# A three-layer interaction network on one core: products made in pairs, one whole group fewer per step

## What is computed

```python
h = x
for i, S in enumerate([128, 128, 128]):
    Wr = Ws[i].reshape(39, h.shape[1], S)
    out = relu(einsum('bfd,bgd,fgs->bsd', x, h, Wr) + bs[i][None, :, None])
    if i != 2:
        h, direct = (out[:, :64], out[:, 64:])
    else:
        direct = out
    outs.append(direct)
return sum(concatenate(outs, axis=1), axis=-1)
```

## Time and profile before

| | us |
|---|---|
| median of 3 runs | 571.18 (571.01 to 573.93) |
| profiled execution, its time | 570.96 |
| its span in the trace | 569.1 |
| PE busy | 558.0 (98%) |
| DVE busy | 531.8 (93%) |
| POOL busy | 505.5 (89%) |
| ACT busy | 365.8 (64%) |
| granted TensorE clock, mean | 0.996 |

### The profile page before, as it was taken

How to read it: one execution, slowest core, us unless ns; L and a number is a source line. 1 busy time by engine, 2 the same in 40 slices (tenths; PEclk the granted TensorE clock), 3 DMA queues, 4 the chain that set the end, 5 groups by cost and what they waited for, 6 DMA issues and landing times.

```text
span 569.1 us, 7814 instructions
## 1 busy us (share of the span) xinstructions
PE 558.0 (98%) x2003; PEld 377.6 (66%) x2003; DVE 531.8 (93%) x516; ACT 365.8 (64%) x409; POOL 505.5 (89%) x222
## 2 busy tenths in 40 slices
PE   8899999999999999999999999999999999999997
PEld 4354666767676666667767667676767766666765
DVE  5679999999999999999999999999999999999975
ACT  1255775766767576676776758586676757668562
POOL 1257999899999999999899999989999999999995
PEclk9899999999999999999999999999999999999999
DMA  8998935738375582846649285573837558262001
GB/s 331 412 413 329 383 115 181 299 124 332 101 261 225 179 332 85 311 157 203 276 146 346 68 295 214 166 313 113 329 111 256 229 173 337 79 210 80 0 2 37
DMA packets 27390, 121.68 MB, mean 214 GB/s; under 512 B 3312, under 2 KB 3440, under 8 KB 25328
## 3 DMA queue, kind: packets, MB, share of 16 engines
q1 hardware_dynamic: 27376, 121.52, 58.8%
HBM read 120.98 MB, written 0.52 MB: 213 GB/s over the span
## 4 chain that ended last, share of the span: by engine, by line
PE 88%; POOL 5%; issue 3%; DMA 1%; DVE 1%; ACT 1%; SPq 0%; POOLq 0%; DVEq 0%; ACTq 0%
PE acc L572 88%; POOL z_lo L294 4%; DMA xfirst<-x 1%; POOL w_lo L540 1%; DVE z_whole L431 0%; DVE z_raw L431 0%; ACT h L660 0%; ACT last L660 0%; ACT z_hi L657 0%; SPq L304 0%; SPq L327 0%; DVE z_hi L292 0%; ACT direct L660 0%; DVE sums L454 0%; DVE z_lo L291 0%
## 5 line engine op out<-in xcount | busy, mean ns | idle before, releaser
L294 POOL TENSOR_TENSOR z_lo<-z_raw,z_hi 128x1024 fp32r<-128x1024 f32 x202 | 477.8, 2406 | 25.2 <-ACT z_hi L657 22.7
L657 ACT CAST z_hi<-z_raw 128x1024 fp32r<-128x1024 f32 (+1 forms) x215 | 216.9, 1022 | 111.5 <-DVE z_raw L431 94.0
L431 DVE TENSOR_TENSOR z_raw<-h,xwide 128x1024 f32<-128x1024 f32 x189 | 225.6, 1214 | 4.7 <-ACT h L660 3.0
L572 PE MATMUL acc<-z_hi,w_hi 128*128 128x512 f32 (+1 forms) x543 | 210.1, 460 | 0.8 <-ACT last L660 0.8
L572 PE MATMUL acc<-z_hi,w_lo 128*128 128x512 f32 x530 | 171.7, 395 | 0.0
L572 PE MATMUL acc<-z_lo,w_hi 128*128 128x512 f32 x498 | 160.0, 397 | 2.3 <-POOL z_lo L294 1.9
L572 PEld LDWEIGHTS acc<-z_hi,w_hi 128*128 128x128 f32 (+1 forms) x543 | 102.2, 188 | 60.6 <-issue 39.5
L572 PE MATMUL acc<-z_whole,w_whole 128*128 128x512 f32 x256 | 120.0, 592 | 0.0
L572 PEld LDWEIGHTS acc<-z_hi,w_lo 128*128 128x128 f32 x530 | 99.4, 188 | 24.0
L572 PEld LDWEIGHTS acc<-z_lo,w_hi 128*128 128x128 f32 x498 | 92.6, 187 | 28.4 <-POOL z_lo L294 5.8
L431 DVE TENSOR_TENSOR z_whole<-h,xwide 128x1024 f32<-128x1024 f32 x68 | 82.3, 1213 | 6.2 <-PE acc L572 3.9
(11 more groups left out here) (25 smaller groups left out, 155.1 us busy)
## 6 DMA issues: line engine op xcount, KB each, us to landing
xwide<-x SPq DMA_DIRECT2D x160, 512.0 KB, 4.7
xfirst<-x SPq DMA_DIRECT2D x13, 2048.0 KB, 7.8
xfirst<-x SPq DMA_DIRECT2D x4, 768.0 KB, 12.2
xwide<-w SPq DMA_DIRECT2D x2, 1024.0 KB, 16.7
xwide<-x SPq DMA_DIRECT2D x1, 1280.0 KB, 11.8
xfirst<-x SPq DMA_DIRECT2D x2, 512.0 KB, 11.4
xwide<-x SPq DMA_DIRECT2D x1, 768.0 KB, 9.2
z_raw<-w0b SPq DMA_DIRECT2D x1, 640.0 KB, 6.0
```

The costliest lines, as they stand in the source:

```text
L294: return eng.tensor_tensor(lo[0:rows, 0:n, :], z[0:rows, 0:n, :], hi[0:rows, 0:n, :].bitcast(F32), ALU.subtract)
L431: nc.vector.tensor_tensor(dst, in0, in1, ALU.mult).then_inc(made[kind], 1)
L572: return nc.tensor.matmul(dst, w[0:rows, place, :], z[0:rows, t - G * g, :], start=first and first_g and t == G * g, stop=final and t == T ...
L657: nc.scalar.copy(z_hi[0:rows, slot("PV", pair, par, pos, HI_RING), 0:n, :], src).then_inc(hi_made, 1)
```

## The change

The order of a step becomes a string in which P groups of one layer stand side by side. Two neighbouring P groups of layer 1 or 2, the first of them with an even count of P groups ahead of it, are multiplied by one DVE instruction of 2048 columns; it waits until both slots of z_raw are free and counts as two. A step now has 5 W, 14 P and 5 V groups: in layer 1 group 12 is whole, 11 is P and 13 is V (before, 11 and 13 were whole and 12 was P); in layer 2 groups 22 and 28 are whole and 25 is V. z_hi has 4 slots instead of 6. The loop body is four steps. The first steps get new orders; layer 0 of block 1 is summed in acc[2] instead of acc[0]; the split of the weights of layer 2 stands on ACT ahead of relu1 of step 1 instead of behind it; the reductions move to positions 6 and 9. On SP the load of layer 2's weights moves one place forward, ahead of the second part of block 2's x, and of the x pieces of layer 1 in step 1 five instead of six go out first. relu2 stays at position 3, relu1 at 0, relu0 at 21.

```diff
+LOOP = 4
-KINDS = ("WPWP", "PWPWPPVPPV", "PPWPVPPWPV") 
+ORDER = "10P 11P 12W 13V 14P 15P 00W 20P 21P 16V 22W 01P 02W 03P 23P 24P 25V 17P 18P 19V 26P 27P 28W 29V"
-SCHEDULE = "111112100122221001212222"
-ORDER_0 = "00W 01W 02W 03W 11W 13W 10W 12W 16W 14P 17W 15P 18P 19V"
-ORDER_1 = ("00W 01W 22W 27W 02W 03W 20P 10P 11W 21P 12P 23P 13W 14P 24V 15P 16V 25P 17P 18P 19V "
-           "26P 28P 29V")
-SPLIT2_AT_1 = 2
-WHOLE_RING, RAW_RING, HI_RING, LO_RING = 4, 4, 6, 4 
+ORDER_0 = "00W 01W 02W 03W 12W 10W 11W 13W 16W 14W 15P 17W 18P 19V"
+ORDER_1 = ("00W 01W 22W 28W 02W 03W 20P 21P 10P 11P 12W 13V 23P 24P 14P 15P 16V 25V 17P 18P 19V "
+           "26P 27P 29V")
+SPLIT2_AT_1 = 0
+WHOLE_RING, RAW_RING, HI_RING, LO_RING = 4, 4, 4, 4 
-SUM1_AT = 7
-SUM2_AT = 8
+SUM1_AT = 6
+SUM2_AT = 9
+def twin(j, pos):
+    these = order(j)[pos:pos + 2]
+    return len(these) == 2 and these[0][2] == these[1][2] == "P" and these[0][0] == these[1][0] > 0 \
+        and these[0][1] + 1 == these[1][1] and before("P", j if isinstance(j, int) else 3, pos) % 2 == 0
...
+                both = 2 if twin(j, pos) else 1
+                n = G * both if both > 1 else len(tiles_of(layer, g))
...
-                    ready(dve, lo_made["P"], number - RAW_RING + 1)
-                    dst = z_raw[0:rows, slot("P", pair, par, pos, RAW_RING), 0:n, :]
+                    ready(dve, lo_made["P"], number + both - RAW_RING)
+                    at = slot("P", pair, par, pos, RAW_RING)
+                    dst = z_raw[0:rows, at:at + both].rearrange("p a g n -> p (a g) n")[:, 0:n, :]
...
-                nc.vector.tensor_tensor(dst, in0, in1, ALU.mult).then_inc(made[kind], 1)
+                nc.vector.tensor_tensor(dst, in0, in1, ALU.mult).then_inc(made[kind], both)
...
-                    products(pair, par, pos)
+                    if not (pos and twin(j, pos - 1)):
+                        products(pair, par, pos)
...
-            with dve.Fori(1, PAIRS - 1) as pair:
-                for par in range(2):
-                    step(pair, par)
+            with dve.Fori(0, (BLOCKS - 4) // LOOP) as turn:
+                for par in range(LOOP):
+                    step(LOOP // 2 * turn + 1, par)
...
-                dst = acc[layer][:, :]
+                dst = acc[2 if isinstance(j, int) and (layer, j) == (0, 0) else layer][:, :]
...
-                    ready(pe, acc_read[layer], j + (1, 0, -1)[layer])
+                    if isinstance(j, int) and (layer, j) == (2, 1):
+                        pe.wait_ge(acc_read[0], 2)
+                    if isinstance(j, int) and layer == 0 and j < 2:
+                        ready(pe, acc_read[0], j)
+                    else:
+                        ready(pe, acc_read[layer], j + (1, 0, -1)[layer])
...
                 if isinstance(j, int) and j == 0:
-                    relu0(j, par)
                     copy_xrep(1)
+                    relu0(j, par % 2)
```

More of the change, by code:

```diff
@@ L20 @@
 PAIRS = BLOCKS // 2
+LOOP = 4
+assert LOOP % 2 == 0 and (BLOCKS - 4) % LOOP == 0
 BB = N // DIM
@@ L31, with groups @@
 TILES = (T0, T12, T12)
-KINDS = ("WPWP", "PWPWPPVPPV", "PPWPVPPWPV")
-G12 = len(KINDS[1])
-SCHEDULE = "111112100122221001212222"
-ORDER_0 = "00W 01W 02W 03W 11W 13W 10W 12W 16W 14P 17W 15P 18P 19V"
-ORDER_1 = ("00W 01W 22W 27W 02W 03W 20P 10P 11W 21P 12P 23P 13W 14P 24V 15P 16V 25P 17P 18P 19V "
-           "26P 28P 29V")
-SPLIT2_AT_1 = 2
-WHOLE_RING, RAW_RING, HI_RING, LO_RING = 4, 4, 6, 4
+ORDER = "10P 11P 12W 13V 14P 15P 00W 20P 21P 16V 22W 01P 02W 03P 23P 24P 25V 17P 18P 19V 26P 27P 28W 29V"
+ORDER_0 = "00W 01W 02W 03W 12W 10W 11W 13W 16W 14W 15P 17W 18P 19V"
+ORDER_1 = ("00W 01W 22W 28W 02W 03W 20P 21P 10P 11P 12W 13V 23P 24P 14P 15P 16V 25V 17P 18P 19V "
+           "26P 27P 29V")
+def groups(text):
+    return [(int(e[0]), int(e[1]), e[2]) for e in text.split()]
+STEP = groups(ORDER)
+KINDS = ["".join(e[2] for e in sorted(STEP) if e[0] == layer) for layer in range(3)]
+G12 = len(KINDS[1])
+SPLIT2_AT_1 = 0
+WHOLE_RING, RAW_RING, HI_RING, LO_RING = 4, 4, 4, 4
 V_LAG = 2
@@ L56 @@
 RELU2_AT = 3
-SUM1_AT = 7
-SUM2_AT = 8
+SUM1_AT = 6
+SUM2_AT = 9
 assert KINDS[1][-1] == KINDS[2][-1] == "V"
[L63 to L74, removed]
 BEGIN = {-1: [(0, g, "W") for g in range(len(KINDS[0]))],
-         0: [(int(e[0]), int(e[1]), e[2]) for e in ORDER_0.split()],
-         1: [(int(e[0]), int(e[1]), e[2]) for e in ORDER_1.split()]}
+         0: groups(ORDER_0),
+         1: groups(ORDER_1)}
 def order(j):
@@ L176 @@
 assert sorted(e[:2] for e in BEGIN[0]) == sorted(e[:2] for e in STEP if e[0] < 2)
-assert len(SPLIT0) > 0 and SPLIT_COUNT[1] <= 16 and SPLIT_COUNT[2] <= 16
+assert len(SPLIT0) > 0 and SPLIT_COUNT[1] <= 20 and SPLIT_COUNT[2] <= 16
 def cin(nc, x, x0, w0a, w0b, w1, w2, w_rest, b, out):
@@ L213, in cin @@
         z_psum = psum("z_psum", [128, G, N])
-        stage = [None, xwide[:, 1, T12 - 4:T12, :].rearrange("p a (b s) -> p (a b) s", s=SIZE),
-                 xwide[:, 1, T12 - 8:T12 - 4, :].rearrange("p a (b s) -> p (a b) s", s=SIZE)]
+        stage = [None, xwide[:, 1, T12 - 5:T12, :].rearrange("p a (b s) -> p (a b) s", s=SIZE),
+                 xwide[:, 1, T12 - 9:T12 - 5, :].rearrange("p a (b s) -> p (a b) s", s=SIZE)]
         xsecond = xwide[:, 1, 0:1 + T0, :]
@@ L263, in cin @@
         for kinds, ring in (("W", WHOLE_RING), ("P", RAW_RING), ("PV", HI_RING), ("PV", LO_RING)):
-            assert 2 * sum(e[2] in kinds for e in STEP) % ring == 0
+            assert LOOP * sum(e[2] in kinds for e in STEP) % ring == 0
         def place_of(j, layer):
@@ L339, in _ @@
             load_first(2, xfirst_head_in[0], range(0, 1 + G))
+            sp.dma_start(stage[2][:, 0:SPLIT_COUNT[2], :], w2).then_inc(w_staged[2], 16)
             load_first(2, xfirst_head_in[1], range(1 + G, 1 + 2 * G))
-            sp.dma_start(stage[2][:, 0:SPLIT_COUNT[2], :], w2).then_inc(w_staged[2], 16)
             load_first(2, xfirst_in, range(1 + 2 * G, 1 + T0))
             sp.wait_ge(*made_all(0, 0))
-            for g in range(G12 - 4):
+            for g in range(G12 - 5):
                 load_wide(1, 1, g)
@@ L352, in _ @@
             sp.wait_ge(w2_lo_made, 1)
-            for g in range(G12 - 4, G12 - 2):
+            for g in range(G12 - 5, G12 - 2):
                 load_wide(1, 1, g)
@@ L376, in products @@
                 layer, g, kind = order(j)[pos]
-                n = len(tiles_of(layer, g))
+                both = 2 if twin(j, pos) else 1
+                n = G * both if both > 1 else len(tiles_of(layer, g))
                 rows = rows_of(layer, G * g)
@@ L409, in products @@
                         dve.wait_ge(h_ready[0], 2 * (j + 1))
-                    dve.wait_ge(xw_in[1 - par][g], 16 * (pair + par + 1))
+                    for each in range(g, g + both):
+                        dve.wait_ge(xw_in[1 - par % 2][each], 16 * (pair + par // 2 + par % 2 + 1))
                     in0 = h[0][:, None, :].to_broadcast([128, n, N])
-                    in1 = xwide[:, 1 - par, G * g:G * g + n, :]
+                    in1 = xwide[:, 1 - par % 2, G * g:G * g + n, :]
                 else:
@@ L416, in products @@
                     in0 = h[1][:, None, :].to_broadcast([128, n, N])
-                    in1 = xwide[:, par, G * g:G * g + n, :]
+                    in1 = xwide[:, par % 2, G * g:G * g + n, :]
                 number = before(kind, j, pos)
@@ L462, in step @@
                 if (not isinstance(j, int) or j > 1) and order(j - 1)[-1][2] == "V":
-                    late.append((V_LAG - 1, pair + par - 1, 1 - par, len(order(j - 1)) - 1))
+                    late.append((V_LAG - 1, *((pair, par - 1) if par else (pair - LOOP // 2, LOOP - 1)), len(order(j - 1)) - 1))
                 for pos, (layer, g, kind) in enumerate(order(j)):
@@ L467, in step @@
                     if pos == SUM1_AT and not (isinstance(j, int) and j < 1):
-                        sum_direct(j - 1, par)
+                        sum_direct(j - 1, par % 2)
                     if pos == SUM2_AT and not (isinstance(j, int) and j < 2):
                         sum_last(j - 2)
-                    products(pair, par, pos)
+                    if not (pos and twin(j, pos - 1)):
+                        products(pair, par, pos)
                     if kind == "V":
@@ L549, in _ @@
                 step(0, par)
-            with pool.Fori(1, PAIRS - 1) as pair:
-                for par in range(2):
-                    step(pair, par)
+            with pool.Fori(0, (BLOCKS - 4) // LOOP) as turn:
+                for par in range(LOOP):
+                    step(LOOP // 2 * turn + 1, par)
             for par in range(2):
@@ L635, in _ @@
                 step(0, par)
-            with pe.Fori(1, PAIRS - 1) as pair:
-                for par in range(2):
-                    step(pair, par)
+            with pe.Fori(0, (BLOCKS - 4) // LOOP) as turn:
+                for par in range(LOOP):
+                    step(LOOP // 2 * turn + 1, par)
```

(16 more changed lines are left out.)

## The result

The changed kernel takes 592.07 us (median of 4 runs, 591.62 to 592.31) against 571.1 before: ratio 1.036, 95% interval 1.033 to 1.039. Its profiled execution has a span of 590.2 us against 569.1. The forecast was 592.

The account below looks back on a forecast made before the run. A loop of waits, 35.1 us per step, bounds the kernel. From 570.96: +4.2 up to step 2, +0.2 first step, +15.0 for 12 steps, +1.0 step 15, +1.0 last step and tail: about 592 us, range 583 to 599.

Parts of the forecast that it names:

- The bound before: In the middle PE is busy for all 33.85 us of a step, DVE needs 33.09; PE bounds by under 1.
- parts 1 and 2: A whole group made V: PE 33.54 us per step; six pairs saving 0.40: DVE 33.82, so no shorter step.
- Part 3, the new waits: Loop in the middle over relu2, copy and subtraction of 13V, pair 23/24, POOL, PE: 35.1 us per step, 1.3 above 33.85.
- Part 4: z_hi's 4 slots: mid-step copies of 17P to 27P wait 0.3 to 1.0 each at no cost; step 1 pays.
- Part 5, the first steps: Layer 2's first product at 41.3 instead of 43.18, yet step 2 begins at 77.2 instead of 72.95: +4.2 us.
- Loop body: Three backward jumps per engine instead of six, costed at nothing.
- A: Ring wait of the pairs (z_raw) alone, relu2 not late: step 33.85 + 0.5, total 583 us; chance 0.13.
- B: DVE alone is the bound, no wait bites: 33.82 us per step, total 569 to 571; chance 0.05.
- C: Faster: PE stays the bound at 33.54 us per step, total 565; chance 0.08.
- D: Hand-offs of 0.2 instead of 0.1, or a code stall at each of three jumps: 597 to 602; chance 0.06.
- E: Pairs fail to form as the change says: 34.2 us of DVE work and over 580; no chance given.

Follow-up runs that it names:

- a_loop12: Changed kernel with a loop body of 12 steps instead of 4, nothing else: 591.2 us, 1.035 of the kernel before, period 34.95.
- a_hi6: Changed kernel with 6 slots of z_hi instead of 4 and a loop body of 12 steps: 589.8 us, 1.033 of the kernel before, period 34.95.
- a_hi6_relu2_4: Changed kernel with 6 slots of z_hi, a loop body of 12 steps and relu2 at position 4: 585.6 us, 1.025 of the kernel before, period 34.35.
- a_relu2_4: Changed kernel with relu2 at position 4 instead of 3, behind the copy of 13V: 595.05 us, 1.042 of the kernel before, period 34.93.
- a_order1: Changed kernel with another order of step 1 alone, no V product following another: 588.7 us, 1.029 of the kernel before, period 35.06.
- b_acc2: Kernel before with layer 0 of block 1 summed in acc[2] instead of acc[0], nothing else: 568.5 us, 0.996 of the kernel before.

## Why the prediction was right, point by point

**The bound before, parts 1 and 2.** No engine's work could carry a gain: right. The pair's pitch is 2.20 and it lasts 2.28, as extrapolated from the two sizes of the earlier trace rows. The rule of the Trainium skill, "VectorE: DVE Perf Modes", section "The DRAIN you can't avoid", as the prediction read it, would have the pitch at 2.28. The same section adds that a next op that is not held starts earlier, which the prediction left out; the trace agrees with that part. The pairs came as costed, and so did the V group's subtraction, but for one thing: a V product that stands right behind a V subtraction follows it after 1.26 (313.17 to 314.43), not 1.13.

**Part 3, the new waits.** The loop was forecast at 35.1 and is 35.05 to 35.06. Term by term, in the timelines above: DVE from 295.58 to 307.49, 11.91 for 12.05; pair 23/24 until POOL starts 3.51 (to 311.00), for 3.53; POOL's six groups 14.22 for 14.15; hand-off to PE 0.05; PE from 325.27 to relu2 at 328.92, 3.65 for 3.7; relu2's pitch 0.58 (to 329.50), as forecast; copy and hand-off 1.13 (to 330.63), for 1.14. They add up to 35.05, from one subtraction of 13V to the next. The waits were 0.71 (0.8) and 0.18 (0.2 to 0.5). So the mechanism was right and not only the sum. That this loop held the step is shown by a_loop12, a_hi6 and a_hi6_relu2_4: with the second loop open, moving relu2 takes 0.60 off the period. That it was the only loop was not so.

**Part 4 was the step that failed.** It said that in the middle z_hi's four slots cost nothing, because POOL is still at work when the copies of 17P to 27P wait. POOL is, and those groups lose nothing by it. What was left out is what stands behind these copies on ACT: relu0, relu1 and the copies of the next step's 10P and 11P. These come late, POOL idles before 10P (1.68 in a_relu2_4), and a second loop closes over PE, ACT and POOL, 34.93 long. On the kernel before, the cut from six slots to four costs 0.84 us per step (b_hi4). In the changed kernel this loop is 0.13 shorter than the one over relu2 and hidden behind it. That the forecast of 592 did not suffer is luck: nothing in the prediction says why the second loop had to be the shorter one. The expectations for the next runs did suffer, a_relu2_4 (586) by 9 us and those with single products by 6 to 8.

**Part 5, the first steps.** First product of layer 2: 41.3 forecast, 41.14. POOL begins: 49.4, 49.17. Subtraction of 16V: 65.3, 65.04. Step 2 begins: 77.2, 76.98. The wait of that subtraction has the cause given only in part: with six slots it is still 1.83 (2.88 with four), as a neighbouring V product forces it ahead of its place; a_order1 shows that the order is the cause.

**Loop body.** Costed at nothing, from 2 steps to 4, which no run measures alone; a body of 12 steps instead of 4 gives 0.1 us per step, 0.9 us of time.

**Rivals.** A, the ring wait alone (583), is the state of a_hi6_relu2_4, and needed two edits to get there. B and C needed waits that don't bite; no kernel without them was found, and PE's 33.54 was never reached. D is out: the hand-offs on the loop are 0.05 to 0.12 (for example 309.77 to 309.88, DVE to ACT), and no step of the loop is more than 0.05 longer than the rest. E is out, for the trace has 93 products of 2048 columns: six in each of steps 1 to 15 and three in the last.

## What to carry to other kernels

When three engines are each about 90% busy or more, the sum of work alone does not give the time: follow the waits once around a step until they close, and add up that loop; here it gave the period to 0.1 us. But look for the second loop as well, since an edit that takes away the longest gives only the distance to the next: here 0.13 us of a possible 0.6. A ring that is cut short delays not only the group that waits for the slot, but all that stands behind it in the same queue. And a view can name the wrong releaser where an instruction waits for two things: look whether the engine named had long been done, as with 14P's copy above. Merging two products saved 0.07 us of fixed cost and cost a later hand-over and a wait for two slots at once, which on this ring of four was more than it saved. And an instruction that waits for another engine (relu2) must not stand in front of one that a third engine needs soon.

## What had not been expected of the hardware

In the kernel before, idle time of 2.19 us on PE was followed by slower matmuls: the 14 after it took 8.16 us instead of 6.0. The granted clock was 0.50 (1.2 GHz) in the stretch from 19 to 21 us and 1.00 from 22 us on. With the idle time gone (b_acc2, and the changed kernel) it stayed at 1.00. An idle time of 1.86 us on PE ahead of 11.00 in b_acc2 had no such effect, and even the one of 2.19 does not have it in every execution: six executions of the kernel before show a mean clock of 1.00 and took 569.2 to 569.5 us, while all others whose clock is on record have 0.997 or less and took 570.8 or more. Against b_acc2's 568.5 this puts about 0.8 us of the 2.5 to the idle time itself and the rest, about 1.6, to the lower clock. This split rests on means over whole executions, for only one of them was traced.

In the changed kernel the period was 0.1 us shorter when the 12 steps stood in one body; what in the longer body does this was not separated.
